# Keys made already turned, and the context loop run over pairs of batches

## The reference

```python
q = (x @ Wq).reshape(B, N, H, D).transpose(0, 2, 1, 3)
kv = (context @ Wkv).reshape(B, M, 2, H, D)
...
q = _per_head_ln(q, qn_w)
k = _per_head_ln(k, kn_w)
attn = jnp.einsum('bhnd,bhmd->bhnm', q, k) * SCALE
attn = jnp.where(mask[:, None, :, :], attn, -jnp.inf)
attn = jax.nn.softmax(attn, axis=-1)
out = jnp.einsum('bhnm,bhmd->bhnd', attn, v)
```

## Time and profile before

| what | value |
|---|---|
| median of 3 runs | 714.97 us (713.3 to 717.66) |
| the profiled execution: time, span | 714.0 us, 712.2 us |
| mean granted TensorE clock | 0.995 |
| TensorE busy | 689.2 us, 97% |
| VectorE, ScalarE, GpSimd busy | 482.7 us (68%), 443.0 us (62%), 314.1 us (44%) |
| SyncE's transfer queue, share of 16 engines | 38.8% |

### The profile page before, as it was taken

One profiled execution on the slowest core, in us unless ns is written; L12 is line 12 of the kernel. 1 busy time (PEld: TensorE's weight loads), 2 busy tenths in 40 slices (PEclk: granted clock), 3 DMA queues, 4 the chain that ended last, 5 costly groups with the idle time before them and its releaser, 6 DMA issues.

```text
span 712.2 us, 14068 instructions
## 1 busy us (share of the span) xinstructions
PE 689.2 (97%) x4651; PEld 566.1 (79%) x4651; DVE 482.7 (68%) x866; ACT 443.0 (62%) x936; POOL 314.1 (44%) x246
## 2 busy tenths in 40 slices
PE   5999999999999999999999999999999889999996
PEld 4677888888887888888878888888788768888875
DVE  7897776766757757667577567956477757655673
ACT  4756785776667757766677656475554455665550
POOL 1553543544434435444344376725910024655625
PEclk9999999999999999999999999999999999999998
DMA  8994342543343424333433306910135367566649
GB/s 253 190 189 123 118 132 82 142 110 111 103 118 95 125 82 139 109 111 103 118 95 97 104 1 192 288 67 0 60 115 196 125 215 193 106 117 109 107 77 344
DMA packets 95063, 91.98 MB, mean 129 GB/s; under 512 B 11440, under 2 KB 68784, under 8 KB 95024
## 3 DMA queue, kind: packets, MB, share of 16 engines
q1 hardware_dynamic: 89728, 79.14, 38.8%
q0 software_dynamic: 4720, 11.27, 8.6%
q10 hardware_dynamic: 576, 1.05, 0.4%
HBM read 71.52 MB, written 19.92 MB: 128 GB/s over the span
## 4 chain that ended last, share of the span: by engine, by line
PE 89%; DVE 4%; DMA 4%; issue 1%; ACT 1%; SPq 0%; DVEq 0%; POOLq 0%; ACTq 0%
PE pK L34 47%; PE pV L34 12%; PE pP L34 9%; PE pV L1728 5%; PE pT L1816 4%; PE pS L1772 3%; PE pP L1800 2%; DMA fin<-total 1%; PE pT L1961 1%; PE pT L1613 1%; DMA big<-x_rows,idx_x 1%; PE pS L1891 1%; DMA total<-big,idx 1%; PE pS L1983 1%; PE pV L1863 1%
## 5 line engine op out<-in xcount | busy, mean ns | idle before, releaser
L34 PE MATMUL pK<-parts 128*128 128x512 f32 x744 | 188.3, 400 | 0.0
L34 PEld LDWEIGHTS pK<-parts 128*128 128x128 f32 x744 | 134.4, 188 | 38.7 <-issue 13.6
L583 POOL TENSOR_TENSOR parts<-big,parts 128x1024 fp32r<-128x1024 f32 x32 | 77.2, 2411 | 118.6 <-DVE p_rem L1251 118.0
L593 POOL TENSOR_TENSOR parts<-ctxR,parts 128x1024 fp32r<-128x1024 f32 x32 | 77.1, 2410 | 94.5 <-ACT parts L726 94.5
L1121 DVE TENSOR_TENSOR kn<-pK,head_rs 128x512 f32<-128x512 f32 x62 | 42.9, 692 | 40.0 <-ACT head_rs L740 40.0
L34 PE MATMUL pK<-w,lhs 128*128 x276 | 69.1, 399 | 0.3 <-DVE lhs L1537 0.2
L1115 DVE TENSOR_REDUCE head_ss<-sq 128x8 f32<-128x512 f32 x62 | 42.5, 685 | 27.8 <-ACT sq L734 27.8
L34 PEld LDWEIGHTS pK<-w,lhs 128*128 128x128 f32 x276 | 50.3, 188 | 10.8 <-issue 1.1
L838 ACT ACTIVATE prob<-s_m,neg_max 128x257 f32<-128x257 f32 x64 | 32.2, 505 | 36.4 <-DVE neg_max L1235 36.4
L34 PE MATMUL pP<-pT,parts 128*128 128x256 f32 x384 | 52.4, 285 | 0.6 <-DVE pT L1262 0.6
L1553 DVE TENSOR_TENSOR w_p<-big,w_p 128x1024 fp32r<-128x1024 f32 x22 | 27.0, 1226 | 37.6 <-ACT w_p L1035 37.6
(11 more groups left out here) (331 smaller groups left out, 1503.1 us busy)
## 6 DMA issues: line engine op xcount, KB each, us to landing
big<-in_ctx_dram SPq DMA_DIRECT2D x32, 512.0 KB, 3.8
big<-in_ctx_dram SPq DMA_DIRECT2D x120, 128.0 KB, 2.7
total<-zero SPq DMA_DIRECT2D x32, 256.0 KB, 4.0
w_raw<-in_L_ffn_w_dram SPq DMA_DIRECT2D x16, 512.0 KB, 6.7
big<-in_L_ffn_w_dram SPq DMA_DIRECT2D x8, 512.0 KB, 5.7
fin<-total SPq DMA_DIRECT2D x8, 512.0 KB, 7.8
total<-big SPq DMA_DIRECT2D x8, 256.0 KB, 2.7
x_rows<-big SPq DMA_DIRECT2D x8, 256.0 KB, 2.0
```

Of the source, the lines that this page charges most:

```text
L34: last = pe.matmul(out, lhs(a, c), rhs(b, c), start=start and c == first and n == 0, stop=stop and c == chunks - 1 and n == 2)
L583: nc.gpsimd.tensor_tensor(ctxN[:, u, LO], ctx_raw[:, u], ctxN[:, u, HI].bitcast(F32), ALU.subtract).then_inc(cn_lo, 1)
L593: nc.gpsimd.tensor_tensor(ctxT[:, u, LO], ctxR[u][:, :, :], ctxT[:, u, HI].bitcast(F32), ALU.subtract).then_inc(ctx_lo, 1)
```

## The change

The loop runs over 16 pairs of batches. Keys come out of TensorE turned: the weights of the product are now a quarter c of the key weights (128 columns), and its 512 columns are the turned contexts of both batches of the pair (`keys(k, c)`, 12 products a quarter, in banks `pK0`, `pK1` by turns). `kn`, its transposes, `k_sum`, `k_root` and `k_norm` are gone. VectorE copies each quarter out (`key_copy`, into `kT_01` or `kT_23`), ScalarE squares it (`square`, into `sqT`), and TensorE adds the squares of a head with 8 products of a 64 by 32 tile of ones over 512 columns (in `scores`, ahead of the scores). The norm is taken on the scores: ScalarE makes the root of 512 columns (`norm_root`, a logarithm and an exponential), VectorE multiplies the scores by it (`normed`, which then masks and takes the maximum). Scores of the pair's two batches stand in two double banks.

In round k TensorE makes the scores of pair p = k-1, quarters 0 and 1 of the keys of pair k, the turn of the first batch's probabilities, quarter 2, `out_tile` in odd rounds, the first batch's context products, the turn of the second batch's probabilities, quarter 3 and the second batch's context products. `ctxT` holds one pair, so ScalarE's `pair_high(k + 1, h)` waits until all four quarters of pair k are made; `rows_high` for pair k stands at the end of ScalarE's round. The low parts of the next pair's context are made in two halves (`pair_low`). SyncE loads the blocks of both batches before the rows of both. The output of the first four tiles has places of its own (`out_first`), and all of the first four `out_high` and `out_low` run at the end.

Of the removed lines the cut below shows two of VectorE's helpers and TensorE's turn of the first keys; the rest of it is new code, in the order GpSimd, ScalarE, VectorE, TensorE, and each engine has a `pair` of its own. The closing round (`main=False`) has projections of the first tiles where the quarters of the keys were.

```diff
...
+            def pair(k, parts=True, far=True, chunks=()):
+                if parts:
+                    ctx_parts(k * 2 - 2, 0)
+                    ctx_parts(k * 2 - 1, 1)
+                pair_queries(k)
+                last_keys(k)
+                low_part("xo", chunks)
+                if far:
+                    for h in range(2):
+                        pair_low(k + 1, h)
...
-            def k_sum(b, t):
-                dve.wait_ge(k_sq, b * MT + t + 1)
-                nc.vector.tensor_reduce(head_ss[:, t], heads(sq[:, t]), AX.X, ALU.add).then_inc(k_ss, 1)
-
-            def k_norm(b, t, reused=True):
-                dve.wait_ge(k_rs, b * MT + t + 1)
-                if reused:
-                    dve.wait_ge(k_t, b * MT + t - 1)
...
-            def key_turn(n):
-                for c in range(C):
-                    last = pe.transpose(pTT[n][:, c, :], kn_x[:, n, c * P:(c + 1) * P], ident[:, :])
-                last.then_inc(k_t, 1)
...
+            def pair_high(k, h):
+                if h == 0:
+                    act.wait_ge(blk_turned, k * 2 + 2)
+                    act.wait_ge(k_mm, k * C)
+                part = slice(2 * h, 2 * h + 2)
+                act.activation(ctxT[:, :, HI, part], ctxR[:, :, part], ACT.Copy).then_inc(ctx_hi, 1)
+            def norm_root(p, u, first=False):
+                if u == 0:
+                    act.wait_ge(ss_mm, p + 1)
+                    if not first:
+                        act.wait_ge(p_rs, p * 2)
+                act.activation(prob[u][:, :, 0:MT * P], pTU[:, :, u * MT * P:(u + 1) * MT * P], ACT.Ln, bias=HEAD_B,
+                               scale=float(D // HD)).then_inc(rs_lg, 1)
+                act.wait_ge(rs_lg, p * 2 + u + 1)
+                act.activation(prob[u][:, :, 0:MT * P], prob[u][:, :, 0:MT * P], ACT.Exp, scale=-0.5).then_inc(rs_set, 1)
...
+            def square(k, c):
+                act.wait_ge(kT_set, k * C + c + 1)
+                act.activation(sqT[:, c].rearrange("p (u n) -> p u n", u=2), (kT_01, kT_23)[c // 2][:, c % 2, :, 0:MT * P],
+                               ACT.Square).then_inc(sqT_set, 1)
...
+            def pair(tile, r, first=False, main=True, far=True, chunks=()):
+                k = tile * 2 + r
+                p = k - 1
+                odd = r == 1
+                norm_root(p, 0, first)
+                norm_root(p, 1, first)
+                exponentials(p, 0)
                 if main:
+                    square(k, 0)
+                exponentials(p, 1)
+                scaled(p, 0)
                 if main:
+                    square(k, 1)
+                scaled(p, 1)
+                turned_high(p, 0)
+                if main:
+                    square(k, 2)
+                if odd and not first:
+                    last_weights(tile)
+                    act.wait_ge(o_mm, tile)
+                z_high(p, 0, 2 * (1 - r))
+                turned_high(p, 1)
+                if main:
+                    square(k, 3)
...
+                if far:
+                    pair_high(k + 1, 0)
+                    pair_high(k + 1, 1)
...
+                z_high(p, 1, 2 * (1 - r) + 1)
...
+                    act.wait_ge(pc_mm, p * 4 + 2)
+                    rows_high(k * 2, 0, k + 1)
+                    act.wait_ge(pc_mm, p * 4 + 4)
+                    rows_high(k * 2 + 1, 1, k + 1)
...
+            def key_copy(k, c):
+                dve.wait_ge(k_mm, k * C + c + 1)
+                ts((kT_01, kT_23)[c // 2][:, c % 2, :, 0:MT * P], pKV[c % 2][:, :].rearrange("p (u n) -> p u n", u=2), 1.0, None,
+                   ALU.mult).then_inc(kT_set, 1)
...
+            def pair(tile, r, first=False, main=True, far=True):
+                k = tile * 2 + r
+                p = k - 1
+                odd = r == 1
...
+                normed(p, 0)
+                if main:
+                    key_copy(k, 0)
+                normed(p, 1)
+                if odd and not first:
+                    dve.wait_ge(p_rt, tile)
+                denominators(p, 0)
+                if main:
+                    key_copy(k, 1)
+                else:
                     out_add(0)
+                denominators(p, 1)
                 if far:
+                    ctx_turn(ctx_blk, 0, k + 2, reused=k * 2 + 2)
                 if main:
+                    key_copy(k, 2)
+                else:
                     out_add(1)
+                turned_low(p, 0)
+                if far:
+                    ctx_turn(ctx_blk, 1, k + 2, reused=k * 2 + 2)
+                if odd and not first:
+                    out_copy(tile - 1)
                 if main:
+                    z_low(p, 0, 2 * (1 - r))
+                turned_low(p, 1)
+                if main:
+                    key_copy(k, 3)
+                else:
                     ln_norm(TILES, x_all[:, 0])
                     out_add(2)
                     bn_scale(0)
...
+            def keys(k, c, first=0, end=C):
+                if c >= 2:
+                    pe.wait_ge(kT_set, k * C + c - 1)
+                return split_products(pe, pKV[c % 2][:, :].rearrange("p (u n) -> p u n", u=2), wk(c), both_ctx, end,
+                                      start=first == 0, stop=end == C, first=first)
...
+            def scores(p, first=False):
+                pe.wait_ge(kT_set, p * C + C)
+                pe.wait_ge(sqT_set, p * C + C)
+                pe.wait_ge(k_rem, p * 2 + 2)
+                pe.wait_ge(q_set, p * 2 + 2)
+                if not first:
+                    pe.wait_ge(p_lo, p * 2)
+                pe.nop(nofuse=True)
+                tiles = [(c, e, slice(e * HD, (e + 1) * HD)) for c in range(C) for e in range(2)]
+                for c, e, half in tiles:
+                    last = pe.matmul(pTU[c * S:(c + 1) * S, e, :], ones[half, 0:S], sqT[half, c, :], start=True, stop=True,
+                                     tile_position=(e * HD, c * S))
+                last.then_inc(ss_mm, 1)
+                for u in range(2):
...
+            def pair(tile, r, first=False):
+                k = tile * 2 + r
+                p = k - 1
+                odd = r == 1
+                scores(p, first)
+                if first:
+                    pe.wait_ge(ctx_lo, k * 2 + 2)
+                else:
+                    pe.wait_ge(ctx_lo, k * 2 + 1)
+                    keys(k, 0, end=2)
+                    pe.wait_ge(ctx_lo, k * 2 + 2)
+                keys(k, 0, first=0 if first else 2).then_inc(k_mm, 1)
+                keys(k, 1).then_inc(k_mm, 1)
+                turn_weights(p, 0)
+                keys(k, 2).then_inc(k_mm, 1)
+                if odd and not first:
                     out_tile(tile - 1)
...
+                weigh(p, 0, copied=tile if odd and not first else None)
+                turn_weights(p, 1)
+                if not odd:
+                    turn_last_weights(p)
+                keys(k, 3).then_inc(k_mm, 1)
+                weigh(p, 1)
...
```

557 lines of the change are left out of this document (241 added, 316 removed).

## The result

The changed kernel took 825.27 us (median of 4 runs, 823.02 to 828.2), the kernel before 715.62 (4 runs, 713.3 to 717.66): a ratio of 1.1536, 95% interval 1.1475 to 1.1596. The profiled execution took 823.05 us, its span 821.3. That is 109 us longer; 74 had been forecast.

The account below looks back on a forecast made before the run. TensorE, busy for 97% of the span, was taken as the bound. Start 64.0 + first round 23.4 + fourteen rounds 398.0 + closing round 26.5 = 511.9, 74.0 us later; 714.0 + 74.0 = 788 us, range 752 to 813.

Parts of the forecast that it names:

- TensorE's work: TensorE's busy time in four batches: key transposes removed, squares' sums added, 1.2 to 2.4 us less, to 46.3.
- Behind quarter 2: TensorE waits after quarter 2: 1.5 us for the low part in even rounds, 3.5 us for `rem_b` in odd ones.
- From quarter 3 to the probabilities of the next pair: Chain through VectorE and ScalarE of 14.0 us, leaving TensorE idle for some 3 us of each round.
- Costed at nothing: GpSimd's products, SyncE's later row loads, the transfers and VectorE's changed work were taken to add no time.
- The round: Even round 25.25 us, odd round 31.6; together 56.85 for four batches against 47.47, +9.4.
- The ends: First scores at 64.0 us, first round 23.4, closing round 26.5; what follows the rounds unchanged.
- The clock falls in the waits: Rival, chance 0.13: TensorE's clock drops in the rounds' waits; 800 us with seven falls, 825 with 22 more.

Follow-up runs that it names:

- number 8: Changed kernel with the moves of number 3, number 4 and number 7 together, second `rows_high` behind `turned_high(p, 0)`, TensorE's order unchanged: 731.32 us.
- number 11: number 9 with ScalarE's `z_high(p, 0)` ahead of the two `pair_high` in even rounds: 701.41 us, ratio 0.9792 to the kernel before.
- number 3: Changed kernel with ScalarE making `rem_b` (`last_weights(tile)`) ahead of `turned_high(p, 0)`: 779.05 us.
- number 4: Changed kernel with VectorE running `turned_low(p, 0)` ahead of its copy of quarter 2, `key_copy(k, 2)`: 800.47 us.
- number 5: Changed kernel with ScalarE's two `rows_high` copies moved into the next round, behind `norm_root(p, 1)` and `scaled(p, 1)`: 819.19 us.
- number 7: number 5 with `normed(p, 1)` ahead of `key_copy(k, 0)` and `square(k, 0)` behind `scaled(p, 0)`: 771.59 us.
- number 2: Changed kernel with 9, 3, 15 and 5 TensorE products without use filling all four named waits of the rounds: 794.0 us.
- number 1: Changed kernel with 15 TensorE products without use ahead of `out_tile` in odd rounds, in the wait for `rem_b`: 809.33 us.
- number 6: Changed kernel with the moves of number 3 and number 4, and `normed(p, 1)` ahead of `key_copy(k, 0)`: 772.01 us.
- number 9: Changed kernel with TensorE's quarters 2 and 3 ahead of the transposes, both context products at the end, other queues following: 709.99 us.

## Why the prediction fell short, point by point

- **TensorE's work** (1.2 to 2.4 us less in four batches, to 46.3). Right: at the upper clock it is 45.5 (number 8), 2.0 less. The squares' sums take 0.88 us a time (272.67 - 271.79), between the bounds of 0.60 and 1.20. It is 44.2 where three quarters of the keys follow one another (number 11).
- **Behind quarter 2.** Right: 1.47 us in even rounds (1.5 forecast), 3.77 in odd ones (3.5). Removing each one's cause removed it (numbers 3 and 4).
- **From quarter 3 to the probabilities of the next pair.** Right in size: 2.3 and 0.7 us idle in a round, where "some 3 us" stood. ScalarE's queue was as walked. What the walk didn't show is that a second chain, quarter 0, its copy, the second normalising, the second exponentials, ends within 0.2 us of the first (numbers 5 and 7). For the forecast that made no difference; for whoever wants the time back it made all.
- **Costed at nothing.** Held: GpSimd, SyncE and the transfers show up only in the 0.7 us that belongs to the 3.
- **The round.** Even: 25.25 forecast, 25.25 measured. Odd: 31.6 forecast, 36.19 measured. This is the step that failed: the forecast held the clock at 1.00 behind the waits that it had itself added. Its terms "quarter 2.83" and "`out_tile` 4.53" were prices at the upper clock, and in the odd round they took 4.6 and 7.2. Filled with other products, the two rounds took 57.13 where 56.85 was forecast (number 2).
- **The ends.** First scores 64.0 forecast, 63.95 measured; first round 23.4 and 23.63; closing round 26.5 and 30.0, of which the third projection (4.33 us instead of 2.9) and the last half of the context products (2.93 instead of 1.5), both at the lower clock, make 2.8. What follows is unchanged (273.8 us to the span's end, before 274.3). The excess over the forecast is 7 x (61.41 - 56.85) = 32 and 3.5 in the closing round: together 35, which is 823 - 788.
- **The rivals.** "The clock falls in the waits" had 0.13, and it is what happened; its upper price, 825, is the measured time. In part that is luck. It priced 22 falls at 1.7 us each, one for each of the 7 long waits and the 15 waits for the probabilities. In the rounds there were 14, two in each odd round, one behind either wait: the first cost the 1.7 (half of 3.41 us), the second 2.8 (half of 5.59). The even rounds, with waits of 2.3 and 1.5 us, kept their clock in this kernel, and the closing round had two falls. The Trainium skill (TensorE: Matmul & The Clock Gate, section "HAM oscillation — how this bites in real kernels") has it that such a loop pays in every turn; the trace of the changed kernel agrees for odd rounds (0.86), and not for even ones (1.00). The argument against the rival, that the gaps lie between dense products, was wrong: the falls stand between dense products here, and in number 2, with the gaps filled, they are gone.

The chance was misjudged for a reason that can be named: the routing stage had already shown a fall behind one wait of 2.35 us, and the forecast itself held waits as long in every round and put 0.69 on the clock staying up.

## What to carry to other kernels

When a change puts waits into a stretch in which TensorE was packed, walk the queues, and then ask of each product behind a wait what it costs at the lower clock; price that case as a forecast, not as a tail. An independent chunk of products covers a chain only where it stands *between* the chain's start and its end: with the other engines' moves alone the same work took 731 us, and 710 or 701 with quarters 2 and 3 ahead of the transposes and the other queues in that order. When one wait is removed and little comes back, look for the instruction on the other queues that is now idle ahead of its turn; it names the second chain.

## What was not expected of the hardware

- Work without use made the kernel faster: 31 us (825.27 to 794.0), and the granted clock of the rounds went from 0.92 to 1.00.
- Taking away a wait of 1.5 us in even rounds took one of the two falls out of every *odd* round (number 4: 0.92 to 0.94 for all).
- Where the clock fell moved from run to run. In the changed kernel it fell in odd rounds only; in number 1 it fell in some rounds of either kind, though rounds of a kind had the same waits; in number 6, whose longest wait in the rounds is 2.8 us, in all seven even rounds and in no odd one. An even and an odd round of number 6:

```profile
250.71:276.41 25.70, 22.09 (x155) 17.76 (x154) 13.41 (x24) 14.46 (x29) 10.26 (x9) 0.93 0.38 102
276.41:305.32 28.91, 25.04 (x233) 20.58 (x233) 14.01 (x25) 16.45 (x34) 10.26 (x9) 1.00 0.34 91
```

- With waits of at most 1.1 us the clock stayed at 1.00 (number 8), and also with one of 1.6 in every second round (number 9). What beside a round's own waits decides was not settled; the runs show that both the wait for the probabilities (number 7) and that for `rem_b` (number 3) have a part.
